# Attention's opening: first maxima from the split keys, loads and splits in another order, and products of ones ahead of them

## The chip, the cores and the metric

The kernel runs on one core of one Trainium2 chip. The metric is the device time of one execution in microseconds. An engine works through its instructions in the order in which they are written; engines wait for one another by semaphores (`wait_ge(sem, n)`, `then_inc(sem)`). SP is the engine whose queue starts most of the DMAs: a wait in it holds back all that is written behind it.

## What is computed

A layer over x (4 batches, 128 tokens, 512 wide) and a context (4, 2048, 512), in three parts; only the first matters here.

```python
x = x + xattn(layernorm(x), ctx, ctx, w_proj, b_proj)   # 16 heads of 32, softmax over 2048 keys
x = x + attn(layernorm(x), ...)                          # gated scan
x = x + ffn(layernorm(x), ...)                           # 8 experts, top 2, and 2 shared
# xattn: scores = q.k / sqrt(32); w = softmax(scores); out = w v; out @ w_proj.T + b_proj
```

## The kernel before

Attention runs over G = 16 groups, each of one batch and four heads (HG = 4). The keys of a group come transposed, as `kt` [128, 4, 512] fp32 (1 MB): partition q*32 + d holds dimension d of key quarter q. fp32 accuracy is had from fp16 products: keys and queries are split into a high part (fp16 of the value, ScalarE: `split_keys`, `queries_high`) and a low one (fp16 of the difference; GpSimd: `split_keys`, `queries_low`; VectorE: `low_parts`, for groups 0 and 2 only). For the products, `stack` (SP) copies the parts by DMA into a stack of 96 rows, high, low, high, six copies of 128 KB for each half of a group (`kstk`; every third group's stack lies in `wst`). Against it stand queries of 96 rows: high, high, low, made by `queries` (TensorE transposes) and `take_queries` (ScalarE). Two rows more hold the shift.

For a group the steps are: 16 products `max_scores(j, k)` [96 rows, 512 keys], each followed by VectorE's `take_max`; `shift(j)` (VectorE) negates the maxima and `shifted(j)` transposes queries and shift (TensorE), `take_shifted(j)` copies (ScalarE); eight steps n = 8i + hs of `scores(n)` (16 products), `exponent(n)` (ScalarE), the pair sum of its two tiles (GpSimd), `denominators(n)` and `values(n)` (TensorE, fp32). The ring of exponents has four places: `exponent(n)` waits for pair sum n - 4 and for the values of n - 4. The order on TensorE is written out by hand: in group i, steps p = 0 to 3 take two scores, four maxima of the next group (`MAXIMA`), the denominators of the pair before and two values; `shifted(i + 1)` stands between p = 2 and p = 3. For group 0 all maxima come first (`for k in range(MB)`), VectorE reduces them in pairs of banks (L775), and a pair has a ring of three.

Keys are loaded two groups ahead into two buffers, values in two buffers (`load_v` waits until the products with the values two groups back are done, `pv_done`). In the loop, ScalarE splits keys i + 3 at p = 0 and 1, GpSimd behind pair sums hs = 3 and 5; in group 0 it is p = 2, 3 and hs = 5, 7, since group 2's keys are split there first. x is loaded in two parts, batch 0 first; the first batch's norm comes ahead of the maxima, the others' (`first_norm(1, B)`, `root(ln1_var, B, 1, B)`) beside them. `root` needs ScalarE's table for Sqrt, the exponents another one, and a change loads a table.

Of the kernel before, what the change touches and what calls it, by code (L numbers as in the profile page):

```python
# [82 lines left out]
def build_program(nc, t, out):  # L83
# [137 lines left out]
    xs_lo = sem("queries_low")  # L221
    qT_ready = sem("queries_transposed")
# [109 lines left out]
    def _(sp):  # L332
        def load_k(j):
            if j >= 2:
                sp.wait_ge(split_lo, j - 1)
                sp.wait_ge(lo_dve, 2 * min(j // 2, 2))
            sp.dma_start(kt[:, j % 2, :, :], t["keysT"][j]).then_inc(kt_in[j % 2], 16)
# [9 lines left out]
        def stack(j, h):  # L347
# [23 lines left out]
        load_k(1)  # L371
        load_v(0)
        stack(1, 0)
        load_k(2)
        stack(1, 1)
        load_k(3)
        load_v(1)
        stack(2, 0)
        stack(2, 1)
        for i in range(G):  # L380
            if i + 4 < G:
                load_k(i + 4)
            if 0 < i < G - 1:
                load_v(i + 1)
# [49 lines left out]
    def _(act):  # L434
        def split_keys(j, h):
            heads = slice(h * HG // 2, (h + 1) * HG // 2)
            if h == 0:
# [72 lines left out]
        for i in range(G):  # L510
            for p in range(HS // 2):
# [12 lines left out]
                if p == 3 and i + 3 < G:  # L524
# [89 lines left out]
    def _(pool):  # L614
        def split_keys(j, a):
            if a % 2 == 0 or j in (0, 2):
# [15 lines left out]
        split_keys(0, HG - 1)  # L632
# [74 lines left out]
    def _(dve):  # L707
# [55 lines left out]
        low_parts(0, 0)  # L763
        low_parts(0, 1)
# [4 lines left out]
        dve.wait_ge(x_in, 16)  # L769
        first_norm(1, B)  # L770
# [613 lines left out]
```

## Time and profile before

| | |
|---|---|
| median of 3 runs | 531.33 us (531.18 to 531.79) |
| profiled execution | 530.95 us, span 529.1 us |
| busy in the span | PE 471.0 us (89%), DVE 407.2 (77%), ACT 326.9 (62%), POOL 275.0 (52%) |
| attention's steady groups | up to about 275 us |
| DMA | 133.97 MB, mean 253 GB/s |

The profile is one execution. PE is TensorE (PEld its weight loads), DVE VectorE, ACT ScalarE, POOL GpSimd, SPq SyncE's queue. L1044 is a line of the kernel. The chain of waits is followed back from the last instruction; "issue" in it is time for which nothing in the profile accounts, such as a wait for a DMA that ended unseen. PE's busy time includes the latency of products that overlap, so a busy PE isn't one at its peak. The granted clock is in parts of 2.4 GHz.

### The profile page before, as it was taken

To read this page: it belongs to the slowest core of one execution; us is meant where nothing else is said; L and a number is where in the kernel's file an instruction comes from. 1 tells how busy PE (TensorE), PEld (TensorE's weight loads), DVE (VectorE), ACT (ScalarE), POOL (GpSimd) and SP (SyncE) were. 2 spreads that over 40 slices of the span, in tenths; PEclk is the share of its full clock that TensorE was granted. 3 is DMA by queue.
4 is the path that set the end of the run, shared out by engine and by line. 5 is a ranking of instruction groups with operands and counts; after the bars stand their busy time and mean duration, and the time that the engine had idled before them with its cause. 6 is when DMAs were issued, how large, how long until landed. Compare 5 with 4: busy or idle time off the path is not lost.

```text
span 529.1 us, 15791 instructions
## 1 busy us (share of the span) xinstructions
PE 471.0 (89%) x6731; PEld 329.8 (62%) x6731; DVE 407.2 (77%) x614; ACT 326.9 (62%) x363; POOL 275.0 (52%) x262
## 2 busy tenths in 40 slices
PE   0469788999999999999998976998999999999994
PEld 0126556667667676766666543844878878787642
DVE  3467477787877887787768888689699999999426
ACT  3327457766766777766667164455678888878320
POOL 2046499899999999999980210481010101010042
PEclk9999799999999999999999995999999999999998
DMA  7886689998899887999989220086999999997134
GB/s 203 243 189 211 173 225 256 253 250 243 239 252 272 263 252 190 243 257 331 285 329 365 103 79 1 23 273 241 417 349 420 418 418 418 416 417 314 41 95 164
DMA packets 29821, 133.97 MB, mean 253 GB/s; under 512 B 6452, under 2 KB 6708, under 8 KB 18996
## 3 DMA queue, kind: packets, MB, share of 16 engines
q1 hardware_dynamic: 25880, 120.38, 70.0%
q0 software_dynamic: 3680, 12.06, 6.3%
q8 instruction: 53, 0.87, 0.7%
q10 hardware_dynamic: 192, 0.52, 0.5%
q14 instruction: 16, 0.13, 0.1%
HBM read 96.77 MB, written 11.01 MB: 204 GB/s over the span
## 4 chain that ended last, share of the span: by engine, by line
PE 54%; DVE 25%; issue 8%; DMA 8%; ACT 3%; POOL 1%; SPq 1%; DVEq 0%; ACTq 0%; POOLq 0%
PE bank L1079 10%; PE bank L1044 10%; DVE ws L790 9%; PE bank L1064 7%; DVE mx L723 7%; PE bank L1088 6%; DMA wst<-in_ffw 5%; PE bank L1147 3%; PE bank L1204 2%; PE bank L1206 2%; PE bank L1205 2%; DMA kstk<-kl 2%; DVE hf L966 1%; DVE hl L971 1%; PE bank L1051 1%
## 5 line engine op out<-in xcount | busy, mean ns | idle before, releaser
L723 DVE TENSOR_REDUCE mx<-bank 128x1 f32<-128x512 f32 x240 | 154.6, 686 | 55.1 <-PE bank L1044 53.0
L477 ACT ACTIVATE pt<-bank 128x1024 f32<-128x1024 f32 x128 | 124.2, 1023 | 60.3 <-PE bank L1064 59.1
L643 POOL TENSOR_TENSOR ps<-pt 128x512 f32<-128x512 f32 x120 | 150.0, 1276 | 5.2 <-PE bank L1088 3.7
L790 DVE SCALAR_TENSOR_TENSOR ws<-wst,ws 128x2048 f16<-128x2048 f32 x51 | 116.7, 2305 | 2.4 <-ACT ws L532 2.2
L532 ACT ACTIVATE ws<-wst 128x2048 f16<-128x2048 f32 x48 | 90.7, 1905 | 8.0 <-DMA wst<-in_ffw 7.8
L618 POOL TENSOR_TENSOR kl<-kt,kh 128x512 f16<-128x512 f32 x58 | 67.7, 1190 | 28.5 <-ACT kh L442 28.5
L1219 PE MATMUL bank<-xt,ws 128*128 128x128 f16 x480 | 81.2, 219 | 0.8 <-DVE hf L966 0.8
L1220 PE MATMUL bank<-xt,ws 128*128 128x128 f16 x480 | 81.2, 219 | 0.0
L1221 PE MATMUL bank<-xt,ws 128*128 128x128 f16 x480 | 81.2, 219 | 0.0
L1044 PE MATMUL bank<-kstk,q 96*128 96x512 f16 x176 | 69.1, 418 | 12.2 <-DMA kstk<-kl 7.7
L1079 PE MATMUL bank<-pt,v 128*32 128x128 f32 x2048 | 70.4, 277 | 3.5 <-issue 3.1
L680 POOL DMA_DIRECT2D ys_rows<-xn x15 | 8.2, 544 | 121.4 <-ACT xn L599 121.4
L1079 PEld LDWEIGHTS bank<-pt,v 128*32 128x32 f32 x2048 | 58.6, 112 | 5.6 <-issue 4.8
L1064 PE MATMUL bank<-q,kstk 98*128 98x128 f16 x704 | 55.9, 225 | 1.7 <-ACT pt L477 1.0
L1064 PEld LDWEIGHTS bank<-q,kstk 98*128 98x128 f16 x704 | 46.5, 101 | 12.9 <-issue 4.4
L1219 PEld LDWEIGHTS bank<-xt,ws 128*128 128x128 f16 x480 | 47.0, 98 | 1.7 <-DVE hf L966 1.7
L1220 PEld LDWEIGHTS bank<-xt,ws 128*128 128x128 f16 x480 | 47.0, 98 | 0.0
L1221 PEld LDWEIGHTS bank<-xt,ws 128*128 128x128 f16 x480 | 47.0, 98 | 0.0
L1088 PE MATMUL bank<-ps,ones 128*32 128x128 f32 x1024 | 42.1, 281 | 1.8 <-POOL ps L643 1.8
L442 ACT ACTIVATE kh<-kt 128x1024 f16<-128x1024 f32 x32 | 33.8, 1063 | 9.6 <-DMA kt<-in_keysT 9.6
L1044 PEld LDWEIGHTS bank<-kstk,q 96*128 96x128 f16 x176 | 16.8, 100 | 36.3 <-DVE mx L723 18.5
L1088 PEld LDWEIGHTS bank<-ps,ones 128*32 128x32 f32 x1024 | 24.4, 110 | 19.1 <-issue 13.8
(173 smaller groups left out, 717.9 us busy)
## 6 DMA issues: line engine op xcount, KB each, us to landing
wst<-in_ffw SPq DMA_DIRECT2D x51, 1024.0 KB, 11.5
kt<-in_keysT SPq DMA_DIRECT2D x16, 1024.0 KB, 5.6
v<-in_vals SPq DMA_DIRECT2D x16, 1024.0 KB, 9.8
kstk<-kh SPq DMA_DIRECT2D x84, 128.0 KB, 4.2
kstk<-kl SPq DMA_DIRECT2D x44, 128.0 KB, 3.4
wst<-kh SPq DMA_DIRECT2D x40, 128.0 KB, 4.2
xs_rows<-biases SPq DMA_DIRECT2D x15, 256.0 KB, 7.8
x_tok<-xs_rows POOLq DMA_DIRECT2D x15, 256.0 KB, 8.6
```

Source lines behind the costliest of these rows:

```text
L477: act.activation(pt[:, n % 4, :, :, :].rearrange("p j a t -> p (j a t)"), bank[:, 2 * (n % 2):2 * (n % 2) + 2, :].rearrange("p j n -> p (j ...
L532: act.activation(ws[:, home_of(q), 0, m, :, :].rearrange("p c n -> p (c n)"), wst[:, q % 2, m, :, :].rearrange("p c n -> p (c n)"), ACT.Co ...
L643: pool.tensor_tensor(ps2[:, n % 4, :, :], pt[:, n % 4, 0, :, :], pt[:, n % 4, 1, :, :], ALU.add)\
L723: dve.tensor_reduce(mx[:, a, q:q + 1], bank[:, 4 + k % 2, :], AX.X, ALU.max).then_inc(m_taken, 1)
L790: dve.scalar_tensor_tensor(ws[:, home_of(q), 1, m, :, :].rearrange("p c n -> p (c n)"), wst[:, q % 2, m, :, :].rearrange("p c n -> p (c n) ...
L1044: pe.matmul(bank[:, home, :], q1[:, j % 2, a, :], stacks[j % 3][0:KS, q, a, :], start=True, stop=True).then_inc(m_ready, 1)
L1064: mm = pe.matmul(bank[:, 2 * (n % 2) + j, a * P:(a + 1) * P], stacks[i % 3][:, tile // 4, a, tile % 4 * P:(tile % 4 + 1) * P], q2[:, i % 2 ...
L1079: mm = pe.matmul(bank[a * HD:(a + 1) * HD, 6 + i % 2, 0:P], v[:, i % 2, tile, a * HD:(a + 1) * HD], pt[:, n % 4, j, a, :], start=(tile == ...
L1088: mm = pe.matmul(bank[a * HD:(a + 1) * HD, 6 + i % 2, P:2 * P], ones[:, :], ps2[:, n % 4, a, :], start=False, stop=(hs == HS - 1), skip_gr ...
L1219: pe.matmul(o, ws[:, home, 0, m, c, part], xt[:, k % 2, c, :], start=(c == 0), stop=False)
L1220: pe.matmul(o, ws[:, home, 0, m, c, part], xt[:, k % 2, C + c, :], start=False, stop=False)
L1221: mm = pe.matmul(o, ws[:, home, 1, m, c, part], xt[:, k % 2, c, :], start=False, stop=(c == C - 1))
```

## The change

- SP: the second keys are loaded right behind the identity, `load_k` and `stack` wait for less, stacks, values and the rest of x are queued in another order, and `load_v(2)`, `stack(3)` and `load_k(4)` go ahead of the loop.
- Group 0's maxima no longer use the stack. `max_pair(0, k)` multiplies from the split keys themselves, with K = 32: three products (high by high, low by high, high by low) for each of two key quarters. The queries for it are repeated over all four quarters (`zw`, made by `wide_high` on ScalarE and VectorE's subtraction), transposed by eight transposes (`wide_queries`) and copied in two halves (`take_wide`).
- VectorE makes all low parts of group 0's keys, GpSimd none; of group 2's VectorE makes half and GpSimd half, earlier.
- The statistics of batches 1 to 3 and their norm go from the opening to group 1, the root with them; `queries_high(4)` and `queries_low(4)` go to group 2.
- ScalarE's splits of keys i + 3 are at p = 2, 3 and GpSimd's behind hs = 5, 7 for groups 0 to 2.
- TensorE computes 20 products of ones (fp32, 128x128) ahead of the wide transposes and 6 ahead of `shifted(0)`; their result isn't used.

```diff
+ROWS = 1
+    wide = wproj.bitcast(F16).rearrange("p n (a z c) -> p n a z c", a=HG, z=2)
+    zw, q0 = wide[:, 0:2, :, :, :], wide[:, 2:4, :, :, :]
@@ SP
         def load_k(j):
             if j >= 2:
-                sp.wait_ge(split_lo, j - 1)
-                sp.wait_ge(lo_dve, 2 * min(j // 2, 2))
+                sp.wait_ge(lo_dve, 2 if j < 4 else 3)
+                if j > 2:
+                    sp.wait_ge(split_lo, j - 2)
         def stack(j, h):
...
-            sp.wait_ge(split_lo, j + 1)
-            if j == 2:
-                sp.wait_ge(lo_dve, 4)
+            if j > 0:
+                sp.wait_ge(split_lo, j)
+            if j in (0, 2):
+                sp.wait_ge(lo_dve, 2 if j == 0 else 3)
         sp.dma_start(idh[:, :], t["idh"]).then_inc(id_in, 16)
+        load_k(1)
...
-        sp.wait_ge(kt_in[0], 16)
-        sp.dma_start(x[:, 1:B, :], t["x"][:, 1:B, :]).then_inc(x_in, 16)
-        sp.wait_ge(split_hi, 2)
-        copies(0, 0, kh, (0, 2 * HD))
-        sp.wait_ge(lo_dve, 2)
-        sp.wait_ge(split_lo, 1)
-        copies(0, 0, kl, (HD,))
-        copies(0, 1, kl, (HD,))
-        load_k(1)
+        stack(0, 0)
+        stack(0, 1)
+        load_k(2)
+        stack(1, 0)
         load_v(0)
-        stack(1, 0)
-        load_k(2)
         stack(1, 1)
         load_k(3)
+        sp.dma_start(x[:, 1:B, :], t["x"][:, 1:B, :]).then_inc(x_in, 16)
+        stack(2, 0)
         load_v(1)
-        stack(2, 0)
         stack(2, 1)
+        load_v(2)
+        stack(3, 0)
+        load_k(4)
+        stack(3, 1)
@@ ScalarE
+                    if j - 2 < ROWS:
+                        act.wait_ge(m_ready, MB * (j - 1))
+        def wide_high(j):
+            q, _ = queries_of(j)
+            act.wait_ge(xn_done, 1)
...
+            act.activation(zw[:, j % 2, :, 0, :].rearrange("p a (r d) -> p a r d", r=HG),
+                           q.unsqueeze(2).broadcast_to([P, HG, HG, HD]), ACT.Copy).then_inc(wide_hi, 1)
+        def take_wide(j):
...
+            act.wait_ge(wq_ready, j + 1)
+            for half in range(2):
+                act.activation(q0[:, j % 2, 2 * half:2 * half + 2, :, :].rearrange("k a z t -> k (a z t)"),
+                               half_bank(6 + (j + 1) % 2)[:, 512 * half:512 * half + 512], ACT.Copy).then_inc(wq_done, 1)
+        root(ln1_var, 1, 0, 1)
+        wide_high(0)
         for h in range(2):
             split_keys(0, h)
-        root(ln1_var, 1, 0, 1)
-        act.wait_ge(split_hi, 2)
-        stack_rows(act, 0, 1, kh, (0, 2 * HD))
+        take_queries(0)
         queries_high(0)
         queries_high(1)
-        take_queries(0)
-        take_queries(1)
-        root(ln1_var, B, 1, B)
-        act.activation(r1[:, 1, 0:2], eps[:, :], ACT.Exp)
         for h in range(2):
             split_keys(1, h)
+        take_queries(1)
+        act.activation(r1[:, 1, 0:2], eps[:, :], ACT.Exp)
         take_shifted(0)
-        exponent(0)
-        exponent(1)
+        for n in range(2):
+            exponent(n)
+            split_keys(2, n)
         queries_high(2)
...
-                if i == 0 and p < 2:
-                    split_keys(2, p)
-                if p in ((2, 3) if i == 0 else (0, 1)) and i + 3 < G:
+                if p in ((2, 3) if i < 3 else (0, 1)) and i + 3 < G:
                     split_keys(i + 3, p % 2)
...
+                if i == 1 and p == 2:
+                    root(ln1_var, B, 1, B)
+                if i == 2 and p == 0:
+                    queries_high(C)
-                if p == 3 and i + 3 < G:
+                if p == 3 and i + 3 < G and i != 1:
                     queries_high(i + 3)
@@ GpSimd
-        split_keys(0, HG - 1)
...
-                if i == 0 and hs == 4:
-                    split_keys(2, HG - 1)
-                if hs in ((5, 7) if i == 0 else (3, 5)) and i + 3 < G:
+                if i == 0 and hs == 1:
+                    for a in (2, 3):
+                        split_keys(2, a)
+                late = 2 * (i < 3)
+                if hs in (3 + late, 5 + late) and i + 3 < G:
...
+                if i == 2 and hs == 1:
+                    queries_low(C)
@@ VectorE
+        dve.wait_ge(wide_hi, 1)
+        dve.tensor_tensor(zw[:, 0, :, 1, :]..., queries_of(0)..., zw[:, 0, :, 0, :]..., ALU.subtract).then_inc(wide_lo, 1)
+        low_parts(0, 0)
+        low_parts(0, 1)
...
+                if i == 1 and p < 3:
+                    dve.wait_ge(x_in, 16)
+                    first_norm(p + 1, p + 2)
+                if i == 1 and p == 3:
+                    dve.wait_ge(roots, 2)
+                    link(dve.reciprocal(lnv[:, 2, 1:B], lnv[:, 0, 1:B]))
+                    first_normed(1)
...
-                if p in (1, 2) and i == 0:
-                    low_parts(2, p - 1)
+                if p == 0 and i == 0:
+                    low_parts(2, 0)
@@ TensorE
+        def wide_queries(j):
+            pe.wait_ge(wide_lo, j + 1)
+            for n in range(2 * HG):
+                mm = pe.transpose(half_bank(6 + (j + 1) % 2)[:, n * P:(n + 1) * P], zw[:, j % 2, n // 2, n % 2, :],
+                                  idh[:, :])
+            mm.then_inc(wq_ready, 1)
+        def max_pair(j, k):
+            a, q = block_of(k)
+            pe.wait_ge(wq_done, 2 * j + a // 2 + 1)
+            pe.wait_ge(split_hi, 2 * j + a // 2 + 1)
+            if k >= 6:
+                pe.wait_ge(m_taken, k - 4)
+            home = k % 6
+            for n, (z, keys) in enumerate(((0, kh), (1, kh), (0, kl))):
+                if n == 2:
+                    pe.wait_ge(lo_dve, a // 2 + 1)
+                for d in range(2):
+                    lanes = slice((q + d) * HD, (q + d + 1) * HD)
+                    mm = pe.matmul(bank[:, home + d, :], q0[lanes, j % 2, a, z, :], keys[lanes, j % 2, a, :],
+                                   start=(n == 0), stop=(n == 2))
+                    if n == 2:
+                        mm.then_inc(m_ready, 1)
...
+            if i < ROWS and hs % (HS // 2) == 0:
+                pe.wait_ge(k_rep[i % 3][hs // (HS // 2)], 16 * 6 * (i // 3 + 1))
...
         pe.wait_ge(ones_set, 1)
         pe.wait_ge(id_in, 16)
+        def keep_busy(count):
+            for _ in range(count):
+                pe.matmul(bank[:, 7, 0:P], one[:, :], one[:, :], start=True, stop=True)
+        pe.wait_ge(one_set, 1)
+        keep_busy(20)
         queries(0)
+        for k in range(0, MB, 2):
+            max_pair(0, k)
         queries(1)
-        for k in range(MB):
-            max_scores(0, k)
+        keep_busy(6)
         shifted(0)
```

## Rows read from the trace of the kernel before

**Rows 1.** Chain of waits, 0 to 75 us: start us, us, what
```profile
12.60 8.68 DMA kstk<-kl
...
52.67 3.63 issue
```

**Rows 2.** Timeline of all engines, opening: start us, us, engine, line, operation
```profile
1.69 0.43 SPq L359 DMA_DIRECT2D idh<-in_idh  x1
5.25 0.18 DVE L718 BATCH_NORM_AGGREGATE mv<-st 128x2 f32<-128x6 f32 x1
6.96 2.00 ACT L442 ACTIVATE kh<-kt 128x1024 f16<-128x1024 f32 x2 [4.71 <-DMA kt<-in_keysT]
13.30 1.08 ACT L454 ACTIVATE q<-bank 96x512 f16<-96x512 f16 x2 [1.00 <-PE bank L1029]
17.99 0.30 ACT L448 ACTIVATE lnv<-mv,eps 128x3 f32<-128x3 f32 x1 [3.61 <-DVE mv L718]
18.30 1.28 ACT L493 ACT_TABLE_LOAD   x1
21.42 7.96 PE L1044 MATMUL bank<-kstk,q 96*128 96x512 f16 x16 [7.73 <-DMA kstk<-kl]
22.54 9.14 DVE L775 TENSOR_REDUCE mx<-bank 128x2 f32<-128x1024 f32 x8 [4.58 <-PE bank L1044]
24.66 2.00 ACT L442 ACTIVATE kh<-kt 128x1024 f16<-128x1024 f32 x2 [4.86 <-DMA kt<-in_keysT]
33.79 1.86 PE L1064 MATMUL bank<-q,kstk 98*128 98x128 f16 x16 [0.78 <-ACT q L461]
```

**Rows 3.** The same timeline, 36 to 75 us
```profile
41.78 1.94 PE L1079 MATMUL bank<-pt,v 128*32 128x128 f32 x32
46.67 1.06 PE L1079 MATMUL bank<-pt,v 128*32 128x128 f32 x32
47.25 1.94 DVE L760 TENSOR_TENSOR kl<-kt,kh 128x1024 f16<-128x1024 f32 x1
56.30 1.01 PE L1044 MATMUL bank<-wst,q 96*128 96x512 f16 x2 [3.63 <-issue]
64.09 2.28 POOL L618 TENSOR_TENSOR kl<-kt,kh 128x512 f16<-128x512 f32 x2 [7.44 <-ACT kh L442]
```

**Rows 4.** TensorE's timeline, the transposes of `shifted` alone
```profile
32.35 0.66 PE L1051 MATMUL bank<-idh,xs 128*98 128x128 f16 x4 [2.97 <-DVE xs L734]
...
52.24 0.42 PE L1051 MATMUL bank<-idh,xs 128*98 128x128 f16 x4
...
74.21 0.42 PE L1051 MATMUL bank<-idh,xs 128*98 128x128 f16 x4
...
92.14 0.42 PE L1051 MATMUL bank<-idh,xs 128*98 128x128 f16 x4
...
138.60 0.42 PE L1051 MATMUL bank<-idh,xs 128*98 128x128 f16 x4
153.58 0.42 PE L1051 MATMUL bank<-idh,xs 128*98 128x128 f16 x4
```

**Rows 5.** GpSimd's timeline in a steady group
```profile
144.19 4.97 POOL L643 TENSOR_TENSOR ps<-pt 128x512 f32<-128x512 f32 x4
149.13 2.28 POOL L618 TENSOR_TENSOR kl<-kt,kh 128x512 f16<-128x512 f32 x2
```

**Rows 6.** VectorE's timeline, the first low parts of keys alone
```profile
8.05 1.23 DVE L760 TENSOR_TENSOR kl<-kt,kh 128x1024 f16<-128x1024 f32 x1 [2.61 <-ACT kh L442]
```

**Rows 7.** Busy times by stretch, with PEclk, DMA share and GB/s at the end, and DMA issues
```profile
0.00:24.00 24.00, 3.63 (x15) 1.78 (x16) 8.13 (x14) 7.26 (x12) 2.71 (x12) 1.00 0.85 238
...
kt<-in_keysT SPq DMA_DIRECT2D x5, 1024.0 KB, 7.7
```

**Rows 8.** TensorE's timeline, fp32 products at the end of attention and in the scan
```profile
299.80 3.17 PE L1147 MATMUL bank<-ao_wproj 128*128 128x512 f32 x7
...
310.21 0.66 PE L1185 MATMUL bank<-scan_uz,wx 64*128 64x512 f32 x1 [0.87 <-ACT scan_uz L560]
310.21 0.69 PE L1186 MATMUL bank<-scan_uz,wx 64*128 64x512 f32 x1
```

More of the change, by code:

```diff
@@ L221, in build_program @@
     xs_lo = sem("queries_low")
+    wide_hi = sem("wide_queries_high")
+    wide_lo = sem("wide_queries_low")
+    wq_ready = sem("wide_queries_transposed")
+    wq_done = sem("wide_queries_copied")
     qT_ready = sem("queries_transposed")
@@ L653, in _ @@
                 pair_sum(HS * i + hs)
-                if i == 0 and hs == 4:
-                    split_keys(2, HG - 1)
-                if hs in ((5, 7) if i == 0 else (3, 5)) and i + 3 < G:
-                    for a in ((0, 1) if hs == (5 if i == 0 else 3) else (2, 3)):
+                if i == 0 and hs == 1:
[3 more added lines that the diff above has]
+                if hs in (3 + late, 5 + late) and i + 3 < G:
+                    for a in ((0, 1) if hs == 3 + late else (2, 3)):
                         split_keys(i + 3, a)
-                if hs == HS - 1 and i + 3 < G:
+                if i == 2 and hs == 1:
+                    queries_low(C)
+                if hs == HS - 1 and i + 3 < G and i != 1:
                     queries_low(i + 3)
@@ L758, in low_parts @@
             dve.wait_ge(split_hi, 2 * j + h + 1)
-            heads = (slice(0, 2), slice(2, 3))[h]
+            heads = slice(2 * h, 2 * h + 2)
             dve.tensor_tensor(kl[:, j % 2, heads, :], kt[:, j % 2, heads, :], kh[:, j % 2, heads, :], ALU.subtract)\
                 .then_inc(lo_dve, 1)
-        low_parts(0, 0)
-        low_parts(0, 1)
         dve.wait_ge(roots, 1)
@@ L778, in _ @@
             take_max(j, k)
-        dve.wait_ge(roots, 2)
-        link(dve.reciprocal(lnv[:, 2, 1:B], lnv[:, 0, 1:B]))
         def scale_win():
@@ L819, in _ @@
                     divide(i - 1)
-                if p == 1 and i in (1, 5, 9):
+                if i == 1 and p < 3:
[5 more added lines that the diff above has]
+                    first_normed(1)
+                if p == 1 and i in (5, 9):
                     first_normed(i // C + 1)
@@ L1023, in _ @@
     def _(pe):
+        def wide_queries(j):
[4 more added lines that the diff above has]
+            mm.then_inc(wq_ready, 1)
         def queries(j):
+            if j < ROWS:
+                wide_queries(j)
+                return
             pe.wait_ge(xs_lo, j + 1)
@@ L1035, in max_scores @@
             if k == 0:
-                pe.wait_ge(q1_done, j + 1)
+                pe.wait_ge(q1_done, j - ROWS + 1)
             if k % (2 * HG) == 0:
                 pe.wait_ge(k_rep[j % 3][k // (2 * HG)], 16 * 6 * (j // 3 + 1))
-            if j > 0:
-                pe.wait_ge(m_taken, MB * j + k - 1)
-            elif k >= 6 and k % 2 == 0:
-                pe.wait_ge(m_taken, k - 4)
-            home = 4 + k % 2 if j > 0 else k % 6
-            pe.matmul(bank[:, home, :], q1[:, j % 2, a, :], stacks[j % 3][0:KS, q, a, :],
-                      start=True, stop=True).then_inc(m_ready, 1)
+            pe.wait_ge(m_taken, MB * j + k - 1)
+            pe.matmul(bank[:, 4 + k % 2, :], q1[:, j % 2, a, :], stacks[j % 3][0:KS, q, a, :],
+                      start=True, stop=True).then_inc(m_ready, 1)
+        def max_pair(j, k):
[3 more added lines that the diff above has]
+            if k >= 6:
+                pe.wait_ge(m_taken, k - 4)
+            home = k % 6
[8 more added lines that the diff above has]
+                        mm.then_inc(m_ready, 1)
         def shifted(j):
             pe.wait_ge(mx_step, 4 * j + 4)
-            pe.wait_ge(q1_done, min(j + 2, G))
+            if j < ROWS:
+                pe.wait_ge(xs_lo, j + 1)
+            following = min(j + 1, G - 1)
+            if following < ROWS:
+                pe.wait_ge(wq_done, 2 * following + 2)
+            else:
+                pe.wait_ge(q1_done, following - ROWS + 1)
             for a in range(HG):
```

22 lines of the change are left out of this document (15 added, 7 removed).

## Prediction

> I write T0, T1, T2 ... for the start of the four transposes of `shifted(0)`, `shifted(1)` ...: once per group of heads, so their distances are the pace of attention.
>
> **What bounds the kernel now.** I read first the chain of waits of the opening, then the timeline beside it, then the starts of `shifted`. TensorE computes nothing but transposes until 21.4 us: the chain runs through 8.68 us of waiting for the stacked low keys [rows 1], while the first keys were split from 7 us on [rows 2]. The eight reductions of the maxima then take 9.14 us [rows 2], a pitch of (9.14 - 1.21)/7 = 1.13 us, 1.21 being one of them. T0 is 32.35, the first scores start at 33.79 [rows 2, 4]. Then the groups take 19.9, 21.95 and 17.9 us, where one takes 14.98 later [rows 4]. In the first of them the chain has 3.63 us in which TensorE waits for group 2's keys [rows 1, 3]; GpSimd stands 7.44 us [rows 3] and works without a break after that. In the steady stretch the maxima's ping-pong between TensorE and VectorE sets the end, but GpSimd is as full: four pair sums take 4.97 and two splits 2.28 us [rows 5], so a group is 8 x 1.24 + 4 x 1.14 = 14.5 us and a small one for the queries. So two things can be won: time until T0, and the 19.9 + 21.95 + 17.9 - 3 x 15.0 = 14.8 us by which the first three groups exceed the pace.
>
> **The opening, step by step.** The second keys are now queued behind the identity; the first 128 KB of x and the first keys keep their place. The mean of x is ready at 5.43 [rows 2]. The root goes ahead of the splits: root, reciprocal and normalisation end near 6.6. `wide_high` copies 128x512, half of what takes 1.0 us [rows 2]: 0.6, until 7.2. ScalarE then splits the first keys, 2.0 us, until 9.2. VectorE makes the wide low parts, half of 1.23 us [rows 6], until 7.9, and then both low halves of the keys, which is one head more than before: 2 x 1.23, until 10.7. GpSimd, which now has no part in this, doesn't disturb it; beside GpSimd the same form took 1.94 [rows 3], so this bound is 12.1.
>
> TensorE, though, can't start the wide transposes at 7.9. `keep_busy(20)` lies ahead of them and begins with the identity's wait, which was over near 7.1 (issued at 1.69 [rows 2], behind keys that came in at 6.96). An fp32 product shows as two passes: the 16 products of two `values` are 32 rows [rows 3]. A pass of 512 columns takes (3.17 - 0.6)/6 = 0.43 us at the high level [rows 8], so a product of 128 columns 0.213, and 0.427 at the low one; 4.3 to 8.5 us for twenty. The first scores ran at the low level, 0.107 us per 128 columns [rows 2]; the busier stretch after them was still low at 41.78 (32 passes in 1.94 us) and high at 46.67 (1.06) [rows 3]. (The granted clock reads 1.00 for the first 24 us [rows 7] though passes there run at 1.2 GHz; in the opening I go by the passes.) From these two rows I take 5 us at 1.2 GHz and the rest at 2.4: 6.8 us, until 13.9. So these products cost about 5 us of wait ahead of the transposes; nothing hides the part beyond 10.7. Eight transposes 0.6, the first half of `take_wide` 0.59 (the copy of 96x512 [rows 2]): 15.1.
>
> A pair of maxima is now six products of K = 32 instead of two of K = 96. The trace has nothing of that shape. The nearest rows are two products of K = 64 on different rows of the array: their passes start together at 310.21 [rows 8]. If the two of a pair overlap so, a pair is 3 x 0.213 = 0.64 us high, 3 x 0.427 = 1.28 low; if they don't, 1.28 and 2.56. VectorE's pitch is 1.13 [rows 2]. I take overlap: the first pair is in at 15.9, the reductions end at 25.1, and T0 = 25.7. At the low level with overlap 1.2 us later. `queries(1)` and `keep_busy(6)`, 1.7 us, and ScalarE's copy with the table load for Exp, 1.28 [rows 2], lie between TensorE's last pair (22.3) and T0: hidden, with half a microsecond to spare. T0 comes 6.6 us sooner.
>
> Ahead of the K = 64 passes the row names nothing but a wait for ScalarE, so I put no price on the change of shape [rows 8]. The Trainium skill speaks against this: TensorEngine Tiling (Array Packing), Key Properties, says that changing the tiling mode drains the array. The kernel goes into K = 32 and out again once; at one whole pass of 0.66 us [rows 8] each, an estimate, that would be 1.3 us and a forecast of 517.8 instead of 516.5.
>
> **Keys and queue.** The stacks of group 0 are now wanted by the scores alone. SP issues them from 9.3 on (each issue some 0.6 us), six for half 0 by 13, twelve by 16.7; the first scores want half 0 at T0 + 1.1 = 26.8. Up to then 3.25 MB follow the second keys. The queues moved 238 GB/s in the first 24 us [rows 7]: 13.7 us, so half 0 of group 1 lies at about 25, just in time. The second keys, until now seen by ScalarE at 24.66 [rows 2], are there before 12. ScalarE splits them at 16.5 to 18.6, since it stands in `take_wide` until TensorE is through with the ones; GpSimd has their low parts by 22.2.
>
> **Group 0**, T0 to T1. Scores at the high level save 0.8 us of 1.86 [rows 2], those behind them about as much. VectorE has one half of `low_parts(2)` in it instead of two parts, earlier, and GpSimd two heads: 1.2 to 1.9 us. ScalarE puts two splits of 1.06 between exponents 0, 1 and 2. The stall of 3.63 us should be gone: the low parts of group 2 are complete at about 37 (GpSimd) and 35.5 (VectorE), not at 53. But the queue carries 7.5 MB from 9.3 on up to group 2's half 0: at 238 GB/s this is there at 41, T1 at the earliest pace at 41.5. I take T1 = 43, 17.3 us of the 19.9.
>
> **Groups 1 and 2.** Here the change puts work in. (a) ScalarE's splits of keys i + 3 go from steps 0, 1 to 2, 3, GpSimd's from behind pair sums 3, 5 to behind 5, 7. In the steady group exponents 6 and 7 end at T + 14.1, and GpSimd's pair sum 5 is done before T + 12.5 if nothing lies before it; it waits 2.5 to 3.5 us for the split, and the pair sums behind it, the exponents four further on and the denominators wait for that. GpSimd has no slack to hide this (14.5 and the queries' 0.4 of 14.98). At nothing hidden 3 us per group; at a lag of GpSimd, as there is after group 0, some of it counts once only. I take 2 us for each. (b) VectorE in group 1: three statistics of 0.85, a reciprocal and a normalisation, 3.4 us against 2.8 of free time; together with (a) nothing to 1 us. (c) ScalarE in group 1: root with a table load and another one back, 2 x 1.28 + 0.3 = 2.9 us [rows 2], right after `take_shifted(2)`; exponent 16 comes 2.9 us after T2 anyway, so about 1 us is seen by it. (d) `load_v(2)` is now ahead of `stack(3)` and waits for all of group 0's products with the values; group 4's keys are queued after it, at about 51, and take 7.7 us to land [rows 7], while ScalarE wants them at 57 to 58: 0 to 2 us. I take T2 = 60 and T3 = 76.5, the latter against 92.14 [rows 4]. From there GpSimd, 8.7 us behind T3 with pair sum 24, is paid at 14.75 a group until the usual lag (144.19 - 138.60 = 5.6 us [rows 4, 5]): T6 = 76.5 + 8.7 + 44.2 - 5.6 = 123.9 instead of 138.60.
>
> **Sum.** 14.7 us: 6.6 before T0, 2.6 in group 0, 5 in group 1, 1.4 in group 2, less 0.9 lag afterwards. Nothing behind attention is touched. The profiled execution took 530.95 (span 529.1 and 1.85 around it), 0.38 below the median of the runs. 530.95 - 14.7 = 516.3; with half of that difference **516.5**.
>
> **Rivals.**
> - *The groups run at the pace at once.* The lag of GpSimd hides (a), and the queue keeps up: T1 = 41.2, T2 = 56.4, T3 = 71.5, gain 22: 509. For it: the load on each engine without the waits fits in 15 us nearly. Against: ScalarE's order is fixed, and group 0 has just this order before, with GpSimd's 7.44 us of standing in it. 0.15.
> - *One stall remains* for want of keys, as the 3.63 us of before with a low clock behind it (32 passes at 1.94 instead of 1.06 [rows 3]), or the pairs don't overlap and the clock is low in them as well (2.56 a pair, T0 = 37, gain 3.4: 527.5). A stall with its clock costs 6: 522.5. Case 521 to 528. For it: the moved waits of (d). 0.2.
> - *Slower:* SP's order. If group 4's keys come late in group 1, split, stack and maxima of the next group are late too, and the delay returns in each group as long as `load_v` stands ahead of `stack`: three times 6 us = 18: 534.5. It decides where these keys land later than about 60. Against: the bytes fit. 0.05.
> - *It doesn't do what it says:* TensorE falls to the low level in the maxima, whose products fill only 0.64 of 1.13 us. Before, products filled 0.85 of 1.13 there and the clock stayed low [rows 2]. With overlap it costs 1.2 us and 1 to 2 in the scores: 519, inside the forecast's own range.
>
> **How the numbers follow.** Forecast, 512 to 521: 0.58; 509 case 0.15; 521 to 528: 0.2; no change 0.02 (within 0.2%, about what a measurement of this kernel can tell); slower 0.05. The range for 8 in 10 takes most of the fast case and half of the next: 508.5 to 525. Faster 0.93, same 0.02, slower 0.05.
>
> **What would show it.** The ones end near 14 and run from 0.43 to 0.21 us a product; the first maxima start at 15, with pairs of K = 32 products starting together; reductions at 1.13 us pitch until 25; T0 at 25.7, T1 43, T2 60, T3 76.5; no standing of TensorE for stacked keys at T1; GpSimd standing for ScalarE's split in groups 1 and 2. A T0 beyond 30, or a pitch of reductions over 1.3, makes the step of the overlap wrong; T3 - T0 under 48 or over 54 makes the groups' step wrong.

## The result and the profile after

The changed kernel takes 524.58 us (median of 6 runs, 521.26 to 526.95); the kernel before took 530.97 (median of 6 runs). The ratio is 0.9895, with a 95% interval of 0.986 to 0.993: faster by 5.6 us by the ratio and 6.4 by the medians, where 14.8 were forecast. The profiled execution took 525.34 us, span 523.5. The ratios leave out executions that took over 1.5% longer than the fastest of their kernel; the profiled one of e4 below is of that kind.

| | before | forecast | after |
|---|---|---|---|
| T0 | 32.35 | 25.7 | 27.03 |
| T1 | 52.24 | 43 | 43.08 |
| T2 | 74.21 | 60 | 61.37 |
| T3 | 92.14 | 76.5 | 83.64 |
| T6 | 138.60 | 123.9 | 131.99 |
| T1 to T6 | 86.4 | 80.9 | 88.9 |

At T1 9.2 us are won, as forecast, and at T6 6.6: the five groups behind the opening take longer than before. This answers to [rows 4] (TensorE's timeline, the transposes of `shifted`: start us, us, line, operation):

```profile
27.03 0.63 PE L1119 MATMUL bank<-idh,xs 128*98 128x128 f16 x4
...
43.08 0.42 PE L1119 MATMUL bank<-idh,xs 128*98 128x128 f16 x4
...
61.37 0.42 PE L1119 MATMUL bank<-idh,xs 128*98 128x128 f16 x4 [0.70 <-DVE xs L767]
...
83.64 0.42 PE L1119 MATMUL bank<-idh,xs 128*98 128x128 f16 x4
...
131.99 0.42 PE L1119 MATMUL bank<-idh,xs 128*98 128x128 f16 x4
```

The opening, timeline of all engines, beside [rows 2]:

```profile
7.85 6.23 PE L1166 MATMUL bank<-one 128*128 128x128 f32 x40 [7.85 <-DMA idh<-in_idh]
...
8.81 2.36 DVE L793 TENSOR_TENSOR kl<-kt,kh 128x1024 f16<-128x1024 f32 x2 [0.18 <-ACT kh L452]
13.92 0.61 PE L1066 MATMUL bank<-idh,ao_wproj 128*128 128x128 f16 x8
15.21 0.60 PE L1104 MATMUL bank<-kh,ao_wproj 32*128 32x512 f16 x4 [0.69 <-ACT ao_wproj L473]
15.66 0.38 PE L1104 MATMUL bank<-kl,ao_wproj 32*128 32x512 f16 x2
15.87 0.59 PE L1104 MATMUL bank<-kh,ao_wproj 32*128 32x512 f16 x4
16.17 9.14 DVE L810 TENSOR_REDUCE mx<-bank 128x2 f32<-128x1024 f32 x8 [5.00 <-PE bank L1104]
...
19.91 1.08 PE L1104 MATMUL bank<-kh,ao_wproj 32*128 32x512 f16 x4
...
21.19 1.08 PE L1104 MATMUL bank<-kh,ao_wproj 32*128 32x512 f16 x4
...
24.36 2.87 PE L1166 MATMUL bank<-one 128*128 128x128 f32 x12
```

Read: VectorE has the low parts at 11.2, but TensorE is in the ones until 14.0, and VectorE stands 5.00 us for the first pair. A pair of maxima takes 15.87 - 15.21 = 0.66 us, later 21.19 - 19.91 = 1.28: two products of K = 32 run side by side at either level. The reductions last 9.14 us as before. The last six products of ones run at the low level, take 2.87 us and let the transposes start 1.1 us after VectorE's shift is done (25.93); with the first pair 0.3 us late that makes T0's 1.3 us over the forecast.

What holds group 2 back stands in ScalarE's timeline at the end of group 1:

```profile
57.86 1.94 ACT L506 ACTIVATE pt<-bank 128x1024 f32<-128x1024 f32 x2 [1.20 <-PE bank L1134]
64.66 1.06 ACT L452 ACTIVATE kh<-kt 128x1024 f16<-128x1024 f32 x1 [4.86 <-DMA kt<-in_keysT]
65.62 0.58 ACT L490 ACTIVATE q<-bank 98x512 f16<-98x512 f16 x1
66.22 1.28 ACT L458 ACT_TABLE_LOAD   x1
67.51 0.30 ACT L458 ACTIVATE lnv<-mv,eps 128x3 f32<-128x3 f32 x1
67.83 1.28 ACT L506 ACT_TABLE_LOAD   x1
69.12 1.94 ACT L506 ACTIVATE pt<-bank 128x1024 f32<-128x1024 f32 x2
```

and in SP's:

```profile
46.07 0.79 SPq L350 DMA_DIRECT2D v<-in_vals  x1
49.12 2.67 SPq L335 DMA_DIRECT2D kstk<-kh  x4
...
53.16 0.53 SPq L345 DMA_DIRECT2D kt<-in_keysT  x1
53.78 3.49 SPq L335 DMA_DIRECT2D kstk<-kh  x4
...
58.65 0.53 SPq L345 DMA_DIRECT2D kt<-in_keysT  x1
72.03 2.42 SPq L335 DMA_DIRECT2D kstk<-kh  x4
```

`load_v(2)` goes out at 46.07 without holding SP up. What holds it is `stack(3, 0)` behind it, which waits until 49.12 for ScalarE's second split of keys 3 (done at 49.10); then its six copies are issued, and group 4's keys only behind them, at 53.16. They land 11.5 us later, at 64.6. ScalarE has stood for them since 59.8. Behind that split are the copy of `take_shifted(2)`, which TensorE had ready at 61.8, the root with two table loads, and exponents 16 and 17, which start 7.75 us after T2, where 2.9 had been counted on. GpSimd stands too, as its timeline shows:

```profile
65.79 2.27 POOL L648 TENSOR_TENSOR kl<-kt,kh 128x512 f16<-128x512 f32 x2 [6.60 <-ACT kh L452]
...
72.08 2.27 POOL L648 TENSOR_TENSOR kl<-kt,kh 128x512 f16<-128x512 f32 x2 [1.40 <-ACT kh L452]
```

The busy times by stretch (PE, PEld, DVE, ACT, POOL; PEclk, DMA share, GB/s) show the same: the DMA engines are full from 44 to 62 us and idle for a third of the next 22, since no stack can be issued between 59.2 and 72.0: SP stands 12.8 us there for ScalarE's split.

```profile
44.00:62.00 18.00, 14.57 (x281) 10.42 (x280) 14.27 (x28) 9.75 (x12) 14.97 (x14) 1.00 1.02 268
62.00:84.00 22.00, 17.02 (x281) 12.08 (x280) 13.33 (x24) 14.83 (x17) 15.16 (x14) 0.84 0.67 166
```

### The profile page after: what moved, and what is told of

The parts are those of the page before. It is cut to its first block, busy times and chain, and to the rows that moved or that the text cites. A ratio compares the mean times of both kernels' runs of the same rounds, so it can differ in the third digit from the quotient of the medians.

```text
span 523.5 us, 15976 instructions
## 1 busy us (share of the span) xinstructions
PE 475.8 (91%) x6819; PEld 336.9 (64%) x6819; DVE 405.5 (77%) x614; ACT 331.1 (63%) x367; POOL 274.7 (52%) x262
## 4 chain that ended last, share of the span: by engine, by line
PE 43%; DVE 21%; DMA 13%; issue 10%; POOL 6%; SPq 4%; ACT 3%; DVEq 0%; POOLq 0%; ACTq 0%
DMA wst<-in_ffw 8%; DVE ws L822 7%; PE bank L1149 7%; PE bank L1089 7%; PE bank L1134 5%; DVE mx L756 5%; PE bank L1158 5%; POOL ps L672 3%; PE bank L1224 3%; SPq L335 2%; DMA idf<-in_idf 2%; POOL kl L648 2%; PE bank L1166 2%; DMA wst<-kl 2%; ACT ws L562 1%
## 5 line engine op out<-in xcount | busy, mean ns | idle before, releaser
L648 POOL TENSOR_TENSOR kl<-kt,kh 128x512 f16<-128x512 f32 x58 | 66.4, 1166 | 11.3 <-ACT kh L452 11.3
L1149 PE MATMUL bank<-pt,v 128*32 128x128 f32 x2048 | 69.0, 275 | 0.7 <-issue 0.7
L1089 PE MATMUL bank<-kstk,q 96*128 96x512 f16 x160 | 60.0, 389 | 4.5 <-DVE mx L756 1.8
L1134 PE MATMUL bank<-q,kstk 98*128 98x128 f16 x704 | 53.4, 219 | 1.7 <-ACT pt L506 1.0
L1134 PEld LDWEIGHTS bank<-q,kstk 98*128 98x128 f16 x704 | 44.1, 98 | 12.2 <-ACT pt L506 3.9
L1089 PE MATMUL bank<-wst,q 96*128 96x512 f16 x80 | 29.7, 384 | 3.9 <-DMA wst<-kl 2.5
```

The lines of the kernel that those rows point to most:

```text
L1089: pe.matmul(bank[:, 4 + k % 2, :], q1[:, j % 2, a, :], stacks[j % 3][0:KS, q, a, :], start=True, stop=True).then_inc(m_ready, 1)
L1134: mm = pe.matmul(bank[:, 2 * (n % 2) + j, a * P:(a + 1) * P], stacks[i % 3][:, tile // 4, a, tile % 4 * P:(tile % 4 + 1) * P], q2[:, i % 2 ...
L1149: mm = pe.matmul(bank[a * HD:(a + 1) * HD, 6 + i % 2, 0:P], v[:, i % 2, tile, a * HD:(a + 1) * HD], pt[:, n % 4, j, a, :], start=(tile == ...
```

## Experiments

Three theories stood against each other: K, the late keys of group 4; S, the splits moved to steps 2 and 3; R, the root and statistics in group 1. A second question was what the ones bring (C, the clock) and cost (O). The executions of one kernel lie 1.6 to 9.9 us apart, so the steps are read in the traces, of which there is one for each kernel, and the verdicts from the ratios to the kernel before. The four kernels of each of the three sets (e1 to e4, e5 to e8, g1 to g4) were run together on one chip, with the kernel before beside them.

| run | T0 | T1 | T2 | T3 | T6 | median | ratio to before (95%) |
|---|---|---|---|---|---|---|---|
| changed kernel | 27.03 | 43.08 | 61.37 | 83.64 | 131.99 | 524.58 | 0.9895 (0.986 to 0.993) |
| e1 | 27.67 | 46.84 | 63.48 | 81.98 | 129.61 | 523.51 | 0.9892 (0.9853 to 0.9932) |
| e2 | 27.51 | 46.68 | 62.66 | 80.16 | 127.92 | 522.2 | 0.9871 (0.9819 to 0.9924) |
| e3 | 26.86 | 42.91 | 61.00 | 79.55 | 124.56 | 519.03 | 0.9824 (0.9771 to 0.9878) |
| e4 | 22.78 | 45.02 | 61.66 | 80.41 | see e4 | 525.63 | 0.9908 (0.9871 to 0.9944) |
| e5 | 27.94 | 43.77 | 71.84 | 87.95 | 133.03 | 526.23 | 0.9947 (0.9917 to 0.9978) |
| e6 | 29.11 | 45.31 | 62.47 | 85.75 | 134.03 | 526.69 | 0.9938 (0.9904 to 0.9973) |
| e7 | 27.58 | 46.61 | 62.58 | 78.95 | 124.38 | 515.58 | 0.9753 (0.9724 to 0.9782) |
| e8 | 31.09 | 46.90 | 63.80 | 80.63 | 127.17 | 522.22 | 0.9868 (0.9833 to 0.9902) |
| g1 | 24.98 | 44.52 | 60.50 | 76.87 | 123.00 | 515.88 | 0.9737 (0.9683 to 0.979) |
| g2 | 26.13 | 45.29 | 61.27 | 77.63 | 122.71 | 515.17 | 0.9712 (0.9672 to 0.9752) |
| g3 | 26.72 | 45.92 | 61.90 | 78.28 | 123.75 | 515.88 | 0.9727 (0.9689 to 0.9765) |
| g4 | 25.59 | 44.44 | 60.42 | 76.78 | 122.81 | 514.65 | 0.9696 (0.9652 to 0.9739) |

**e1_k4_first: group 4's keys ahead of `load_v(2)`.**

```diff
         stack(2, 1)
+        load_k(4)
         load_v(2)
         stack(3, 0)
-        load_k(4)
         stack(3, 1)
```

> Group 4's keys are issued right behind stack(2,1), ahead of load_v(2) and stack(3,0); nothing else differs from the changed kernel. Theory K (late keys): in the changed kernel these keys are issued at 53.2 us and land at 64.7; ScalarE stands 4.9 us for them in step 2 of group 1, and take_shifted(2), the root with its two table loads and exponents 16 and 17 are queued behind. Issued near 46 they land near 56 to 58, the stand goes, and T3 - T2 falls from 22.3 us to 17.5 to 18.5: 3.8 to 4.8 us faster than the changed kernel. Theory S (the splits moved to steps 2 and 3): GpSimd stands for ScalarE's splits whether the keys are there or not; less than 1.5 us is won. Theory R (root in group 1): less than 1.5 us.

ScalarE's timeline at the same place:

```profile
61.79 1.06 ACT L452 ACTIVATE kh<-kt 128x1024 f16<-128x1024 f32 x1
63.94 0.60 ACT L490 ACTIVATE q<-bank 98x512 f16<-98x512 f16 x1 [1.09 <-PE bank L1119]
64.55 1.28 ACT L458 ACT_TABLE_LOAD   x1
65.85 0.30 ACT L458 ACTIVATE lnv<-mv,eps 128x3 f32<-128x3 f32 x1
66.16 1.28 ACT L506 ACT_TABLE_LOAD   x1
67.46 1.94 ACT L506 ACTIVATE pt<-bank 128x1024 f32<-128x1024 f32 x2
```

The stand is gone, the exponents start at T2 + 4.0 instead of 7.75, and T3 - T2 is 18.5 instead of 22.3: what theory K said, 3.8 us. The keys, issued at 46.58, took 9.3 us and were there at 55.9, before the 59.8 at which ScalarE wanted them in the changed kernel; so the stand would have gone with an early T1 too. The ratio doesn't show the 3.8 us (0.9892 and 0.9895, each with an interval of some 2 us to either side); in the time as a whole the keys' place shows only in e3 against e5 below. In this profiled execution T1 came 3.8 us later, for a reason that has nothing to do with the edit, which takes effect at 46 us only. 0.6 of it was there at T0, the rest is the clock; the rows are PEclk of the changed kernel and then of e1 (same columns as above):

```profile
24.00:28.00 4.00, 3.66 (x20) 3.45 (x20) 1.86 (x6) 2.38 (x4) 0.00 (x0) 0.50 1.03 255
28.00:32.00 4.00, 2.62 (x24) 1.45 (x25) 2.29 (x4) 3.26 (x5) 0.00 (x0) 0.98 1.06 291
```

```profile
28.00:32.00 4.00, 3.02 (x21) 1.93 (x19) 0.64 (x2) 2.51 (x4) 0.00 (x0) 0.50 1.04 272
...
36.00:40.00 4.00, 4.00 (x45) 2.40 (x43) 3.22 (x5) 1.05 (x2) 4.00 (x3) 0.50 0.90 267
```

In both, TensorE runs at 1.2 GHz in the last maxima; in the changed kernel's execution it is at 2.4 from 28 us on, in e1's only from 40. With the same instructions up to there, T1 - T0 is 16.05 us in the one and 19.17 in the other. The traces fall into these two kinds: 15.8 to 16.2 (changed kernel, e3, e5, e6, e8) and 18.8 to 19.5 (e1, e2, e7, g1 to g4, and e4, where 22.24 us hold a stand of 2.89). e1 and e3, whose kernels don't differ before T1 and which ran on one chip, are of different kinds: a low clock in group 0 costs 3.1 us, and the kernel doesn't settle which it is.

**e2_norms_early: x, statistics and root back in the opening**, `queries_high(4)`, `queries_low(4)` and `first_normed(1)` where the kernel before has them.

```diff
@@ SP
         load_k(1)
+        sp.dma_start(x[:, 1:B, :], t["x"][:, 1:B, :]).then_inc(x_in, 16)
...
         load_k(3)
-        sp.dma_start(x[:, 1:B, :], t["x"][:, 1:B, :]).then_inc(x_in, 16)
@@ VectorE
         low_parts(0, 1)
+        dve.wait_ge(x_in, 16)
+        first_norm(1, B)
@@ ScalarE
         take_queries(1)
+        root(ln1_var, B, 1, B)
...
-                if i == 1 and p == 2:
-                    root(ln1_var, B, 1, B)
```

> The rest of x is loaded right behind the second keys; statistics of batches 1 to 3 stand on VectorE between its low parts and the maxima, root, reciprocal, first_normed(1) and the queries of group 4 are back where the kernel before has them. Theory K: ScalarE still stands for group 4's keys, the two table loads behind it (2.9 us with the root) go: T3 earlier by 2 to 3 us, and nothing is lost in the opening, since VectorE stands from 11.2 to 16.2 there; x puts 0.75 MB ahead of the stacks (about 3 us of the queue), which has some 1 to 2 us of effect on groups 0 and 1. Sum: 1 to 2 us faster than the changed kernel. Theory R: the root and VectorE's statistics are the whole of the loss in group 2: 4 to 6 us faster. Theory S: within 1 us.

ScalarE still stands for the keys, 2.48 us, since they land at 64.2 again and T1 is 3.7 us later. T3 is 80.16, 3.5 us before the changed kernel's, on a T1 that is later: a little more than K allowed for, less than R asked for. T0 is 0.5 us later than the changed kernel's and no later than that of e1, which has the opening unchanged: the statistics cost nothing there that shows.

**e3_k4_splits: e1 and the splits at steps 0 and 1 from group 1 on.**

```diff
@@ beside the edit of e1
-                if p in ((2, 3) if i < 3 else (0, 1)) and i + 3 < G:
+                if p in ((2, 3) if i < 1 else (0, 1)) and i + 3 < G:
-                late = 2 * (i < 3)
+                late = 2 * (i < 1)
```

> As e1_k4_first, and the splits of keys i + 3 are at steps 0 and 1 (ScalarE) and behind pair sums 3 and 5 (GpSimd) from group 1 on, as in the kernel before. Theory S: 2 to 5 us faster than e1_k4_first, as GpSimd no longer stands in groups 1 and 2. Theory K: ScalarE now wants group 4's keys at T1 + 7 = 50 us, where they can't be (issue near 46 and 8 to 11 us of landing): it stands 5 to 8 us in group 1 instead, and this kernel is 0 to 3 us slower than e1_k4_first.

ScalarE's timeline in group 1, and then GpSimd's first pair sums behind T3, in e1 and in this run:

```profile
54.56 1.06 ACT L452 ACTIVATE kh<-kt 128x1024 f16<-128x1024 f32 x1 [3.50 <-DMA kt<-in_keysT]
```

```profile
90.46 4.97 POOL L672 TENSOR_TENSOR ps<-pt 128x512 f32<-128x512 f32 x4
```

```profile
85.15 4.97 POOL L672 TENSOR_TENSOR ps<-pt 128x512 f32<-128x512 f32 x4
```

Both said something right. ScalarE stands 3.50 us for the keys in group 1 (K, which had 5 to 8), T1 to T3 is 36.6 us against 35.1 in e1. But from T3 to T6 it takes 45.0, the steady pace at once, where e1 needs 47.6 and the changed kernel 48.35 (S). With the late splits GpSimd comes to group 3's pair sums 8.5 us behind T3 (90.46 - 81.98, and as much in the changed kernel), here 5.6 us behind it (85.15 - 79.55), as in the steady groups. The debt is paid over three groups, 2.6 us, and that is more than the 1.5 lost in front. The rest of T6's 5.1 us against e1 is the earlier T1.

**e5_splits_only: the same without the keys' earlier issue**, the fourth corner.

> The changed kernel with the splits of keys i + 3 at steps 0 and 1 (ScalarE) and behind pair sums 3 and 5 (GpSimd) from group 1 on; the queue's order as in the changed kernel. With e1_k4_first and e3_k4_splits this is the fourth corner. Theory K: group 4's keys land at 62 to 65 us, and ScalarE now stands for them in step 0 of group 1, behind exponents 10 and 11, that is from 51 us on: 11 to 13 us of standing, T2 at 70 to 72, T3 not before 86, T6 at 131 to 133; within 1.5 us of the changed kernel or slower by up to 2. Theory S: the late splits alone are the loss, and this is as fast as e3_k4_splits, T6 near 125.

```profile
64.00 1.06 ACT L452 ACTIVATE kh<-kt 128x1024 f16<-128x1024 f32 x1 [12.09 <-DMA kt<-in_keysT]
```

T2 is 71.84, T3 87.95, T6 133.03, all as K said. e3 and e5 differ in the place of the keys' load alone (they ran on two chips, each against the kernel before) and both had the high clock in group 0: T6 is 8.5 us apart, and the ratios are 0.9824 (0.9771 to 0.9878) and 0.9947 (0.9917 to 0.9978), with intervals that don't touch. That is theory K shown in the whole time. The late splits, then, are what kept ScalarE from running into keys that weren't there, and they cost 2.6 us where the keys come in time.

**e7_all: e3 and e2 together.**

> e3_k4_splits and e2_norms_early together: group 4's keys early, splits at steps 0 and 1, norms, statistics and root in the opening. If the costs are separate ones, T3 - T1 is 3 to 4 us less than in e3_k4_splits (36.6), as the root's 2.9 us and VectorE's statistics leave group 1, and T6 is 121 to 122 with T1 at 43: 2 to 3 us faster than e3_k4_splits. If the keys' landing sets groups 1 and 2 whatever stands on ScalarE, it is the same as e3_k4_splits within 1 us.

T1 to T3 is 32.3 us against 36.6 in e3, and T6 124.38 although T1 is 46.61. Part of this is the late T1 itself: ScalarE stands 0.98 us for group 4's keys, where it stood 3.50 in e3. That is 2.5 of the 4.3 us; 1.8 are left for the root, the table loads and the statistics, less than the 3 to 4 expected. The two costs are separate in part only. The ratio is 0.9753; all six runs lie between 514.8 and 516.4. Here groups 1 to 5 take 77.8 us, where the changed kernel takes 88.9.

**e4_no_ones: the changed kernel without its 26 products of ones.**

```diff
-        keep_busy(20)
...
-        keep_busy(6)
```

> The changed kernel without its 26 products of ones. The wide transposes start near 8.7 us instead of 13.9, and TensorE runs at 1.2 GHz until a busy stretch has raised it. Theory O (the ones cost): pairs of maxima take 1.28 us at the low level, T0 is 22.6 to 23.5 instead of 27.0; but stacks and keys of group 1 come with the queue, so T1 falls by 1 to 3 us only and the whole is 0 to 2 us faster than the changed kernel. Theory C (the clock is what the ones bring): scores and values of group 0 at the low level cost 3 to 5 us, T1 is not earlier than 43, and the whole is 1 to 3 us slower.

Chain of waits:

```profile
22.78 0.66 PE bank L1119 x4
...
24.18 1.87 PE bank L1134 x16
26.05 2.89 issue
28.93 0.60 PE bank L1089
```

T0 is 22.78: without the ones the maxima begin 4.3 us sooner and run at the low level, 1.28 us a pair, 9.59 us for the reductions instead of 9.14. 2.89 us then go by before the first product with group 1's stacked keys, and the low clock takes the rest (16 passes of the scores in 1.87 us, 1.05 at the high level; the column PEclk reads 1.00 in this stretch of this trace all the same): T1 is 45.02, between the changed kernel's 43.08 and e1's 46.84. The ratio, 0.9908 (0.9871 to 0.9944), can't be told from 0.9895. In this trace one instruction of VectorE took 7.17 us at 123.28 where its like takes up to 1.3, so its T6 isn't compared.

**e6_ones_between: two more products of ones behind each pair of maxima.**

```diff
         for k in range(0, MB, 2):
             max_pair(0, k)
+            keep_busy(2, 6)
```

(the second number is the bank)

> The changed kernel with two more products of ones (0.43 us at the high level) behind each pair of maxima, into another bank; a pair with them fills 1.07 of the 1.13 us of a reduction. Theory C (the clock decides T1): in the traces so far TensorE's clock was low from about 18 us on; where it was high again at 28 T1 is 43, where it stayed low until 40 T1 is 46.8. With the ones between it stays high in the maxima, keep_busy(6) takes 1.4 instead of 2.9 us, T0 is 25.9 and T1 41.5 to 42.5; the runs lie closer together and 1 to 3 us lower than those of the changed kernel. Rival (the products between get in the way): reductions at a pitch over 1.13, T0 after 27, slower by 1 us or more.

The clock stays high, and the rival is right all the same:

```profile
20.62 0.60 PE L1104 MATMUL bank<-kh,ao_wproj 32*128 32x512 f16 x4
21.07 0.38 PE L1104 MATMUL bank<-kl,ao_wproj 32*128 32x512 f16 x2
21.37 0.71 PE L1166 MATMUL bank<-one 128*128 128x128 f32 x4
21.58 1.23 DVE L810 TENSOR_REDUCE mx<-bank 128x2 f32<-128x1024 f32 x1 [0.17 <-PE bank L1104]
22.02 0.60 PE L1104 MATMUL bank<-kh,ao_wproj 32*128 32x512 f16 x4
```

A pair with its ones has a pitch of 1.40 us, not 1.07: 0.75 from the pair to the ones instead of 0.66, and 0.65 from the ones to the next pair instead of 0.43. T0 is 29.11, 1.2 us of that because the first pair came so much later in this execution, and T1 - T0 is 16.2.

**e8_all_ones: e7 with 22 ones ahead of the identity's wait, 3 behind the wide transposes and 2 behind each pair.**

> e7_all, with the ones where they cost nothing: 22 ahead of the identity's wait (from 1.3 us on, done near 8), 3 behind the wide transposes, 2 behind each pair, 6 ahead of shifted(0) as before. Theory: transposes start at 8.7 instead of 13.9, the reductions at 11.5 to 12, T0 is 21.5 to 22.5 at the high level; group 0 then stands for the stacked keys of group 1 (2.9 us in e4_no_ones), so T1 is 40 to 41, and the whole is 2 to 3 us faster than e7_all. Rival: the queue sets T1 and all behind it; the same as e7_all within 1 us.

Wrong: T0 is 31.09 and the ratio 0.9868, 6 us behind e7. VectorE's statistics, which wait for x, put the reductions off to 15.0; TensorE stood 1.43 us for them, and from 17.98 on the low level was back, with pairs and ones between them taking 2.55 us:

```profile
16.33 0.61 PE L1096 MATMUL bank<-kh,ao_wproj 32*128 32x512 f16 x4 [1.43 <-DVE mx L807]
17.08 0.97 PE L1157 MATMUL bank<-one 128*128 128x128 f32 x4
17.98 1.03 PE L1096 MATMUL bank<-kh,ao_wproj 32*128 32x512 f16 x4
...
20.53 1.03 PE L1096 MATMUL bank<-kh,ao_wproj 32*128 32x512 f16 x4
```

Not all of the 6 us is explained by this. With the high clock in group 0 its T1 (46.90) is that of e7 (46.61); 2.8 us are there at T6, and the profiled executions differ by as much again behind T6. Why stays open.

**g1_all_no_ones, g2_all_ones_first, g3_all_no_last6, g4_ones_first_stack: e7 without any ones; with the 20 ahead of the identity's wait; without the last six; and g2 with `stack(1, 0)` ahead of `load_k(2)`.**

```diff
@@ g2
         pe.wait_ge(ones_set, 1)
-        pe.wait_ge(id_in, 16)
...
         keep_busy(20)
+        pe.wait_ge(id_in, 16)
@@ g4, also
-        load_k(2)
         stack(1, 0)
+        load_k(2)
```

> e7_all without any product of ones. Theory O (where the keys no longer hold the later groups back, the ones cost what they take): T0 22.8 as in e4_no_ones, 2.9 us of standing for group 1's stacked keys, group 0 at the low level until 38 to 40, T1 at 45 and so the same or 1.5 us before e7_all (T1 46.6, there too with a low clock): the same as e7_all to 1.5 us faster. Theory C: e7_all's median rests on executions with a high clock in group 0 (T1 43), then this one is 1 to 3 us slower.

> e7_all with its 20 products of ones ahead of the identity's wait: they start at 1.2 instead of 7.9 us, where TensorE has nothing to do, and are over before 8. The transposes start at 8.7 to 9.1 instead of 13.9; reductions end at 21 to 22.5, T0 is 22 to 24. Theory O: 0 to 1.5 us faster than e7_all, as group 0 stands for the stacked keys. Theory C: the clock is low again before the scores, T1 45 to 46.5: the same as e7_all within 1 us.

> e7_all without keep_busy(6). In the traces with a low clock at 24 us these six take 2.87 us and end 1.1 us after VectorE's shift. Theory O: T0 25.9 to 26.5 instead of 27.6, about 1 us faster. Theory C: they are what raises the clock by 28 us in some executions (T1 43); without them group 0 is always at the low level, T1 at 45 to 46.5, and the median is 0 to 2 us slower.

> g2_all_ones_first with stack(1, 0) ahead of load_k(2) in SP's queue, so that 1 MB less lies ahead of the keys that group 0 waits for. Theory: the 2.9 us of standing go, T1 falls by 2 to 3 us against g2 (41 to 43) and the sum by 1 to 3 us, if group 2's keys, now 0.75 MB later, still land before ScalarE's first split of them (T0 + 2.5). Rival: they don't, ScalarE stands at 26 us for 2 to 3 us, and it is the same as g2 within 1 us.

All four were at the low level in group 0 (T1 - T0 of 18.8 to 19.5) and lie within 1.3 us of one another and of e7 in the median. Without a single product of ones the ratio is 0.9737, with them 0.9753: where the later groups are in order, the ones neither win nor lose what can be measured. In g3 T0 falls by 0.9 us without the last six, as O said, and T1 by 0.7. In g1 and g2 T0 didn't fall to 22 to 24; VectorE's statistics stand before the reductions there and wait for x. g4 has the lowest ratio, 0.9696 (0.9652 to 0.9739), which its interval doesn't set apart from g2's 0.9712. Its theory failed: g2 has no stand for stacked keys in group 0 that could go, and T1 is 0.9 us earlier, not 2 to 3.

## Why the prediction was wrong

**Right: the opening.** The root and normalisation ended at 7.2 (6.6), the ones at 14.1 (13.9), the first pair came to VectorE at 16.17 (15.9), and the pairs overlap (0.66 us against 0.64). T0 missed by 1.3 us, because the clock was low again at 24 us and the last six products of ones, counted at 1.7 us with the copy as hidden, took 2.87.

The rival "it doesn't do what it says" came in this part: the clock fell in the maxima, the reductions kept their pitch, and only the ones behind them were late.

**Right in the sum, by luck of the execution: group 0.** T1 was forecast at 43 and came at 43.08. But the executions are of two kinds, and e1 with the same instructions came at 46.84. I priced the low clock at 1 to 2 us in group 0; it is 3.1.

**Wrong: step (d), the keys of group 4.** I wrote that they are queued at about 51 and take 7.7 us to land, and gave 0 to 2 us for it. Issued at 53.16, they took 11.5, and the stand was 4.9 us. Both halves were off: the issue, because SP was held by `stack(3, 0)`'s wait for ScalarE and not by `load_v(2)`, which I had named; and the landing. The 7.7 was a median of five loads that took 5.1 to 10.1 us in the trace before; here the DMA engines were full (share 1.02). The count of bytes by which I placed the stacks would not have been enough: carried on to these keys, 12 MB from 9.3 us on at 238 GB/s give 59.7, which is late against the 57 to 58 at which I had ScalarE want them, but 5 us short of 64.6. e1 shows the step in the trace (T3 - T2 falls from 22.3 to 18.5), e3 against e5 in the whole time. By the prediction's own sign, T3 - T0 over 54, the groups' step was wrong: it is 56.6.

**Wrong: what stands behind a wait.** I took (c), the root with its table loads, as seen with 1 us, since exponent 16 comes 2.9 us after T2 anyway. This holds only if ScalarE is free at T2. In e1 it is (exponents at T2 + 4.0, 1.1 over that). In the changed kernel the copy of `take_shifted(2)` comes 3.8 us late, and exponent 16 starts 2.9 us behind its end; in e2, where ScalarE stands too but has no root there, it starts 0.7 us behind it. So the root was seen with 2.2 us, not 1. The terms were added as if each had its own cover, though they queue on one engine.

**Right in kind, too dear: (a).** The splits were priced at 2 us for each of groups 1 and 2, with a debt of GpSimd that makes T3 to T6 47.4 us, 2.5 over the pace. The debt was right: GpSimd was 8.5 us behind T3, where I had 8.7, and e1 and e3 show 2.6 us from T3 to T6. The 4 us ahead of T3 were not: there e1 takes less than e3 (35.1 us from T1 against 36.6). Its sign there hung on (d): with late keys the late splits save more than they cost (e5).

**The change of shape on the array.** I put no price on it. e6 makes it eight times over: a pair and two ones take 1.40 us, and 0.66 + 0.43 = 1.09 by themselves, so going from one kind of product to the other and back costs 0.3 us. The Trainium skill (TensorEngine Tiling (Array Packing), Key Properties) says that a change of the tiling mode drains the array; the 0.3 us fits this in kind, though no run changes the shape and nothing else. At 0.3 us for the one such pair of changes, where the prediction had an estimate of 1.3, it moved nothing that could be seen here.

**The rivals.** "One stall remains for want of keys", with (d) as its reason and 521 to 528 us, is what came: 524.58. It had 0.2. The larger stall wasn't where TensorE waits for a stack, as I had it (2.49 us, in group 1), but where ScalarE waits for the keys themselves. "Slower" didn't come, although its condition did (keys later than about 60: 64.6): the delay didn't return in each group, and after T3 only 3.4 us were lost to the pace of 15.0. Of the 14.7 us forecast at T6, 6.6 came. The 8.1 missing are 1.3 before T0, less 1.25 that group 0 gave back in this execution, 1.3 in group 1 (TensorE waited 2.49 us there for the second half of group 2's stack), 5.8 in group 2 and 0.95 from T3 to T6, where GpSimd took 15.15 us a group instead of 14.75 ((137.59 - 92.13)/3 in its timeline). One more is lost from T6 to the end of the profiled execution; that stretch takes 389.1 to 393.0 us in the traces here (390.5 in the kernel before), so it says nothing.

## What to carry to other kernels

When an opening is shortened, the loads behind it are wanted sooner by the same amount. For each load, ask first when it is issued, that is which wait ahead of it in SP's own order ends last, and then take the landing time of loads that were issued while the DMA engines were full (here 9 to 11.5 us for 1 MB), not a median over loads of both kinds (7.7). Compare the sum with the time at which the in-order engine reaches its wait. A table load, a root or a copy that is moved behind such a wait loses part of its cover. Products of ones for the clock are worth a trial without them, as in g1.

## What was not expected of the hardware

- The same instructions ran with TensorE's clock high from 28 us in one execution and from 40 in another; 3.1 us in a single group. What settles it stays open.
- Products of ones between the pairs didn't always hold the high level: in e8 TensorE stood 1.43 us at 14.9 among pairs and ones and was at 1.2 GHz from about 18 on; in e6, with pairs and ones and no stand, it stayed at 2.4 up to T0. These are single traces.
- In the changed kernel the load of 1 MB of keys took 5.1 to 11.5 us to land; the longest one was the one that counted.
